# Windowed attention, first layer: score blocks of up to 256 columns two to a PSUM bank, with one exponential and one mask matmul for both

## The reference, cut to what matters

```python
# layer 0, x: (8, 512, 128)
xn = layernorm(x)
q, k, v = split(xn @ w_in.T + b_in)                 # 16 heads of 8
scores = q @ k.T / sqrt(8)                          # per head, 512 x 512
scores = where(|i - j| <= 128, scores, -1e30)
ctx  = softmax(scores) @ v
x = x + (xn + ctx @ w_out.T + b_out) + int8_matmul(xn, weight_q)
# layer 1: attention with softmax over queries, and a top-2 mixture of 8 experts
```

## Time and profile before

| | |
|---|---|
| Median of 3 runs | 592.09 us (590.72 to 592.15) |
| Span of the profiled execution | 629.5 us |
| TensorE busy in it | 526.0 us (84%) |
| VectorE busy | 442.5 us (70%) |
| ScalarE busy | 352.7 us (56%) |
| GpSimd busy | 307.6 us (49%) |
| First layer's slots, in the trace | 52 us to 353 us |

### The profile page before, as it was taken

One profiled execution on the slowest core, in us unless ns is written; L12 is line 12 of the kernel. 1 busy time (PEld: TensorE's weight loads), 2 busy tenths in 40 slices (PEclk: granted clock), 3 DMA queues, 4 the chain that ended last, 5 costly groups with the idle time before them and its releaser, 6 DMA issues. The chain is left out here.

```text
span 629.5 us, 17819 instructions
## 1 busy us (share of the span) xinstructions
PE 526.0 (84%) x5987; PEld 339.2 (54%) x5987; DVE 442.5 (70%) x1888; ACT 352.7 (56%) x995; POOL 307.6 (49%) x361
## 2 busy tenths in 40 slices
PE   5489998999999999998899898777770899999990
PEld 4124344444444444453444565555550899999890
DVE  6598898798988988887692357677564566555552
ACT  2254777777777777777477545445423145455450
POOL 6572636447465584550101054466644066666562
PEclk9555999999999999999599998778875999999997
DMA  4836073473725548174002070001111133445434
GB/s 104 178 101 135 20 175 81 119 136 87 166 74 145 112 120 163 35 174 92 18 20 59 14 290 25 31 31 34 47 35 59 47 97 89 139 137 161 117 85 124
DMA packets 51385, 61.04 MB, mean 97 GB/s; under 512 B 10001, under 2 KB 42133, under 8 KB 49696
## 3 DMA queue, kind: packets, MB, share of 16 engines
q1 hardware_dynamic: 45824, 50.26, 32.8%
q0 software_dynamic: 4320, 8.47, 4.0%
q10 hardware_dynamic: 1152, 1.18, 0.6%
HBM read 31.68 MB, written 28.39 MB: 95 GB/s over the span
## 5 line engine op out<-in xcount | busy, mean ns | idle before, releaser
L678 DVE CUSTOM_DVE_ANT_0 A<-A,band 128x320 f32<-128x320 f32 (+2 forms) x512 | 213.9, 464 | 46.6 <-PE A L855 45.7
L531 ACT ACTIVATE Pb<-SB 128x320 f32<-128x320 f32 (+2 forms) x512 | 180.5, 401 | 83.3 <-PE SB L891 78.8
L855 PE MATMUL A<-Ks,Qs 48*64 48x320 bf16 (+2 forms) x1024 | 132.7, 311 | 19.1 <-DVE mneg L678 15.9
L882 PE MATMUL SB<-Qs,Ks 50*64 50x320 bf16 (+2 forms) x1024 | 134.7, 300 | 4.7 <-ACT Pb L531 4.1
L855 PEld LDWEIGHTS A<-Ks,Qs 48*64 48x64 bf16 x1024 | 48.9, 108 | 122.3 <-DVE mneg L678 96.3
L1773 POOL DMA_INDIRECT results<-y,xt x71 | 75.9, 1069 | 60.9 <-issue 36.8
L891 PE MATMUL SB<-ends,ident 64*64 64x64 bf16 (+1 forms) x1024 | 102.0, 209 | 1.2 <-issue 1.2
L1224 POOL DMA_INDIRECT expert_rows<-pay,pos x64 | 62.1, 970 | 71.9 <-DVE pay L1407 48.6
L904 PE MATMUL PV<-Pb,Va 128*32 128x320 f32 (+2 forms) x1024 | 87.8, 416 | 0.4 <-ACT Pb L531 0.4
L1892 PE MATMUL l_S<-xT,wt 128*128 128x128 f32 x568 | 82.1, 288 | 2.3 <-ACT xT L1781 1.8
L1892 PEld LDWEIGHTS l_S<-xT,wt 128*128 128x128 f32 x568 | 68.7, 191 | 10.2 <-ACT xT L1781 2.4
(11 more groups left out here) (263 smaller groups left out, 821.6 us busy)
## 6 DMA issues: line engine op xcount, KB each, us to landing
Qs<-parts_dram SPq DMA_DIRECT2D x14, 384.0 KB, 6.0
Ks<-parts_dram SPq DMA_DIRECT2D x14, 384.0 KB, 9.6
xt<-expert_rows SPq DMA_DIRECT2D x71, 65.0 KB
yb<-results SPq DMA_DIRECT2D x7, 512.0 KB
parts_dram<-qp SPq DMA_DIRECT2D x16, 192.0 KB, 2.9
parts_dram<-kp SPq DMA_DIRECT2D x14, 192.0 KB, 2.8
xb<-in_x SPq DMA_DIRECT2D x8, 256.0 KB, 3.1
parts_dram<-qp SPq DMA_DIRECT2D x16, 128.0 KB, 2.8
```

Of the source, the lines that this page charges most:

```text
L531: act.activation(Pb[:, group % 4, c, 0:w], SB[k % NB_BANKS][:, 0:w], ACT.Exp).then_inc(act_exp, 1)
L678: nc.vector.tensor_tensor_reduce(scores_of, scores_of, band[:, skip:skip + w], -1.0, 3e38, ALU.add, ALU.min, mneg[:, step % 2, col:col + 1 ...
L855: mm = nc.tensor.matmul(A[k % NA_BANKS][out:out + HP, 0:w], Qs[b % RING][rows, a, HP * sub:HP * sub + HP], Ks[b % RING][rows, a, lo:lo + w ...
L882: nc.tensor.matmul(out[r0:r0 + HP, 0:w], Ks[b % RING][rows, a, HP * sub:HP * sub + HP], Qs[b % RING][rows, a, lo:lo + w], start=True, stop ...
```

## The change

Blocks of up to 256 columns (`sub` 0, 1, 6, 7; half of all slots) share a bank two by two: the even slot writes columns 0 to `w`, the odd one `w` to `2w`. The masks of both are added by one matmul per half of the partitions, behind the odd slot's scores, and ScalarE takes one exponential of 384 or 512 columns. A **fill** is now what a bank holds (one block or two); the semaphores `pe_B` and `act_exp` count fills, 24 in a step instead of 32.

```diff
+def paired(sub):
+    return reach(sub)[1] <= 256
+
+def fills_to(group):
+    step, sub = divmod(group, NS)
+    return STEP_FILLS * step + sum(HG // 2 if paired(i) else HG for i in range(sub))
+
+def fill_of(k):
+    group, c = divmod(k, HG)
+    return fills_to(group) + (c // 2 if paired(group % NS) else c)
...
         def exp(b, u):
...
-            act.wait_ge(pe_B, k + 1)
-            if c == 0 and group >= 4:
+            fill, w = fill_of(k), reach(group % NS)[1]
+            two = paired(group % NS)
+            if two and c % 2 == 0:
+                return
+            act.wait_ge(pe_B, fill + 1)
+            if c == int(two) and group >= 4:
                 act.wait_ge(pe_PV, group - 3)
-            w = reach(group % NS)[1]
-            act.activation(Pb[:, group % 4, c, 0:w], SB[k % NB_BANKS][:, 0:w], ACT.Exp).then_inc(act_exp, 1)
+            bank = SB[fill % NB_BANKS]
+            if two:
+                act.activation(Pb[:, group % 4, c - 1:c + 1, 0:w], bank[:, 0:2 * w].rearrange("p (n w) -> p n w", n=2),
+                               ACT.Exp).then_inc(act_exp, 1)
...
         def scores(b, u):
...
-            if k >= NB_BANKS:
-                pe.wait_ge(act_exp, k - NB_BANKS + 1)
+            if fill >= NB_BANKS and not second:
+                pe.wait_ge(act_exp, fill - NB_BANKS + 1)
...
-                nc.tensor.matmul(out[r0:r0 + HP, 0:w], Ks[b % RING][rows, a, HP * sub:HP * sub + HP],
-                                 Qs[b % RING][rows, a, lo:lo + w], start=True, stop=True)
+                nc.tensor.matmul(out[r0:r0 + HP, at:at + w], Ks[b % RING][rows, a, HP * sub:HP * sub + HP],
+                                 Qs[b % RING][rows, a, lo:lo + w], start=not second, stop=True, skip_group_check=second)
+            if two and not second:
+                return
...
+                if two:
+                    both = out[rows, 0:2 * w].rearrange("p (n w) -> p n w", n=2)
+                    end = 1 if sub < 2 else 0
+                    ends = both[:, :, w - HP:w] if sub < 2 else both[:, :, 0:HP]
+                    masks = ends16[rows, end].unsqueeze(1).to_broadcast([HP, 2, HP])
...
         def attend(step, sub):
-            pe.wait_ge(act_exp, HG * (group + 1))
+            pe.wait_ge(act_exp, fills_to(group + 1))
```

More of the change, by code:

```diff
@@ L54 @@
 NX = 6
+STEP_FILLS = 24
 def reach(s):
@@ L233, in load @@
             if g >= RING:
-                sp.wait_ge(pe_B, SLOTS * (g - RING + 1))
+                sp.wait_ge(pe_B, STEP_FILLS * STEPS * (g - RING + 1))
             for which, tile, stored in ((0, Qs, dma_pq), (1, Ks, dma_pk)):
@@ L526, in exp @@
             group, c = k // HG, k % HG
-            act.wait_ge(pe_B, k + 1)
-            if c == 0 and group >= 4:
-                act.wait_ge(pe_PV, group - 3)
-            w = reach(group % NS)[1]
-            act.activation(Pb[:, group % 4, c, 0:w], SB[k % NB_BANKS][:, 0:w], ACT.Exp).then_inc(act_exp, 1)
+            fill, w = fill_of(k), reach(group % NS)[1]
[4 more added lines that the diff above has]
+            if c == int(two) and group >= 4:
+                act.wait_ge(pe_PV, group - 3)
+            bank = SB[fill % NB_BANKS]
+            if two:
+                act.activation(Pb[:, group % 4, c - 1:c + 1, 0:w], bank[:, 0:2 * w].rearrange("p (n w) -> p n w", n=2),
+                               ACT.Exp).then_inc(act_exp, 1)
+            else:
+                act.activation(Pb[:, group % 4, c, 0:w], bank[:, 0:w], ACT.Exp).then_inc(act_exp, 1)
         def evac_pv(step):
@@ L869, in scores @@
             lo, w = reach(sub)
+            fill, two = fill_of(k), paired(sub)
+            second = two and c % 2 == 1
             if u % UNITS == 0:
                 pe.wait_ge(dma_m, 32 * (k // UNITS + 1))
-            if k >= NB_BANKS:
-                pe.wait_ge(act_exp, k - NB_BANKS + 1)
+            if fill >= NB_BANKS and not second:
+                pe.wait_ge(act_exp, fill - NB_BANKS + 1)
             if k == 0:
@@ L878, in scores @@
                 pe.wait_ge(dve_const, 10)
-            out = SB[k % NB_BANKS]
+            out = SB[fill % NB_BANKS]
+            at = w if second else 0
             for r0 in (0, HP):
                 rows = slice(r0, r0 + HROW)
-                nc.tensor.matmul(out[r0:r0 + HP, 0:w], Ks[b % RING][rows, a, HP * sub:HP * sub + HP],
-                                 Qs[b % RING][rows, a, lo:lo + w], start=True, stop=True)
+                nc.tensor.matmul(out[r0:r0 + HP, at:at + w], Ks[b % RING][rows, a, HP * sub:HP * sub + HP],
+                                 Qs[b % RING][rows, a, lo:lo + w], start=not second, stop=True, skip_group_check=second)
+            if two and not second:
+                return
             for r0 in (0, HP):
                 rows = slice(r0, r0 + HP)
-                if 1 < sub < NS - 2:
+                if two:
[3 more added lines that the diff above has]
+                    masks = ends16[rows, end].unsqueeze(1).to_broadcast([HP, 2, HP])
+                else:
                     ends = out[rows, 0:8 * HP].rearrange("p (n w) -> p n w", w=4 * HP)[:, :, 0:HP]
                     masks = ends16[rows]
-                else:
-                    ends, masks = (out[rows, w - HP:w], ends16[rows, 1]) if sub < 2 else (out[rows, 0:HP], ends16[rows, 0])
                 mm = nc.tensor.matmul(ends, ident16[rows, rows], masks, start=False, stop=True, skip_group_check=True)
@@ L1005, in _ @@
         pe.wait_ge(dma_later, LATER)
-        pe.wait_ge(act_exp, SLOTS * NB)
+        pe.wait_ge(act_exp, STEP_FILLS * NSTEP)
         tail["projections"]()
```

## The result

The changed kernel takes 586.26 us, the median of 4 runs (585.73 to 587.04), against 592.05 us (590.72 to 592.15) for the kernel before: a ratio of 0.9887 with a 95% interval of 0.9853 to 0.9921. The prediction was 586.1 us.

What follows compares the result with a forecast made beforehand. VectorE sets the pace, except where TensorE comes late with the next block. Terms of 2.1, 1.3, 1.0, 1.1 and 0.4 us sum to 5.9, rounded to 6: 592.1 becomes 586.1 us, range 582.2 to 589.8.

Steps and rivals of the forecast that it cites:

- The price of a pair: ScalarE's exponentials: a pair of 256 columns takes 599 ns, of 192 takes 493, by a line of 0.83 ns a column.
- Slots 4 to 11, 2.1 us: Batches 0 to 6: slot 11's `piece` comes 0.42 us earlier into VectorE's idle time; 2.1 us in all.
- The discount for the load: Slot 16's `Qs` and `Ks` load: in three batches only 0.15 of the 0.42 us is kept.
- The sign I gave: Slot 16: the wait of `piece` for `Ks` comes in more batches than three.
- The rival that it binds everywhere: The load at slot 16 binds in all batches, the first term is gone, 588.2 us; 12%.
- Slots 29 to 40, 1.3 and 1.0 us: Around the q and k copies: `qp` comes 0.21 us earlier (six batches), one exponential less ahead of `kp`, 0.2 (five).
- The last 48 slots, 1.1 us: Stretch without `piece`: scores no longer wait for a bank, `attend` waits for longer exponentials; 1.1 us gained (0.3 to 2.5).
- Masks, 0.4 us: Two mask matmuls fewer per pair, on the path only ahead of slots 4 and 27: 0.4 us (0 to 1.5).
- The slower rival: `attend` waits for the longer exponentials at each of 64 groups of pairs, 13.4 us lost, 599.5 us; 5%.
- The sign that I gave for being wrong: `attend` waiting for `Pb` more than before would show the prediction wrong.
- The sum: Terms 2.1 + 1.3 + 1.0 + 1.1 + 0.4 = 5.9 us, rounded to 6, giving 586.1 us.
- The clock rival: Batch 6's stretch at the lower clock goes, 582.5 us (11%), or another such stretch comes, 589.7 us (4%).

Runs made afterwards that it cites:

- The order on ScalarE alone: Kernel before, with exponentials of blocks up to 256 columns run two together at the odd slot, no shared bank: 594.10 us, ratio 1.0004.
- `e_only_4_7`: Blocks paired only at slots 4 to 7, all other slots as in the kernel before: 591.87 us, ratio 0.9998.

## Why the prediction was right, point by point

**What bounds the kernel.** VectorE sets the pace and stands only where TensorE comes late: right. Its work did not change, its stops did, by 0.82 us a batch.

**The price of a pair.** 601 and 490 ns against 599 and 493, so the line from the earlier trace rows holds to 512 columns, and the fixed part that two cost more than one is 0.19 us at 256 columns (2 x 393 - 601 ns). In the Trainium skill, "ScalarE: Activation LUTs", section "Rules for kernel authors", the fixed part is about 0.3 us, but for an ACTIVATE whose bias is a column of 128 values. The trace agrees: `qp` and `kp`, 512 columns with such a bias, take 0.69 and 0.72 us, 0.27 and 0.29 beside 512 x 0.83 ns. The exponentials have no such bias, and that price is none of theirs.

**Slots 4 to 11, 2.1 us.** 0.38 us measured in a batch (slot 11's stop), 0.39 by the kernel that pairs only there, against 0.42. The order on ScalarE alone gives it too (0.43 us left at slot 11), so here the mechanism is the one forecast. The discount for the load was mostly not needed. I kept 0.15 us in three of seven batches because the load of `Ks` was last at slot 16. It is still last there in two batches, and VectorE doesn't stop for it. (VectorE's stop of 0.80 us at slot 16 of batch 2 is behind TensorE's stop at 135.51, which ends 1.1 us after the load's last piece at 134.45.) The sign I gave, that the wait for `Ks` would come in more batches than three, was wrong. The rival that it binds everywhere is out.

**Slots 29 to 40, 1.3 and 1.0 us.** `project` of k waits 0.21 us less (0.37 to 0.16), and slot 40's stop is 0.19 shorter, against 0.21 and 0.2. The kernel that pairs only there gives 0.43 for both. The explanation was half of it, and this is the step that the prediction had wrong though its sizes fit: it put both terms down to ScalarE's shorter queue, but with the order alone slot 34's stop grows from 0.22 to 0.39 and slot 40's from 1.13 to 1.25. They need the shared bank too.

**The last 48 slots, 1.1 us.** 1.16 measured. The waits moved as forecast: those of the scores for an exponential fell from 9.1 to 4.2 us, those of `attend` rose from 1.3 to 3.6. 0.44 of the 1.16 goes when the pair is two exponentials, and the order alone gives none of it.

**Masks, 0.4 us.** A steady batch with own masks is 0.03 to 0.23 us longer in its batches and the last 48 slots 0.14 shorter. That allows 0 to 1 us in all; the median, 1.9 us above the changed kernel's, says more, with overlapping intervals. The 0.4 us is neither shown nor refuted.

**The slower rival**, `attend` waiting for the longer exponentials: `attend`'s weight loads wait 3.6 us for pairs and 3.8 for single ones in the whole kernel, 7.4 in all against 5.5 before. The sign that I gave for being wrong, that `attend` waits for `Pb` more than before, is there, but with 1.9 us and not 13.4, and 2.3 us more of such waits stand in the last 48 slots, where the forecast had counted them; a steady batch has less of them (0.4 us, 0.5 before).

**The sum.** 5.9 us was forecast and 5.8 measured, and that it is this close is partly luck. Batches 1 to 5 at 0.82, undisturbed, and the last 48 slots at 1.16 are 5.3 us. Batch 0 gave nothing, where 0.63 was forecast: beside the second profile of before, 35.37 and 35.34. There slot 11's stop did not shrink (0.54 and 0.62 us), and what slot 34's lost (0.61 to 0.40) slot 43's gained (0.36 to 0.59); why is open. In place of it came things that the sum did not hold, of both signs: the stop of 1.4 to 1.9 us in batch 1 (in the second profile with 3.4 us at half clock behind it) is no longer there, batch 6 is 1.6 to 4.1 us shorter, and stops for `l_xall` take 2.15 and 1.05 us in batches 3 and 4 and the stop at 135.51 1.2 in batch 2. In the second session the same two kernels were 8.0 us apart.

The clock rival named one of these: batch 6, the one with a stretch at the lower level, got shorter. That stretch is still there, though, and the change doesn't account for its length: 13.6 us in the first profile of before, 6.8 in its second, 6.8 in both of the changed kernel. With the statistics moved the pairs alone are worth 0.72 us in batch 6 (34.46 and 33.74). Of the 3.86 us between the first profiles the stop for `l_xall` is 1.43 (2.23 and 0.80), which leaves 1.7 for the shorter stretch; of the 1.80 between the second ones it is 0.85 (1.71 and 0.86). The window of the stretch in the changed kernel:

```profile
296.60:303.40 6.80, 6.71 (x76) 3.01 (x72) 4.67 (x26) 3.73 (x9) 2.94 (x6) 0.50 0.01 2
```

Such a stretch of 3.4 to 13.6 us begins at the end of the stop for `l_xall` or up to 4.6 us later in batch 6 of all eleven profiles whose statistics stand at slot 28, and in the three whose statistics moved batch 6 has none.

## What to carry to other kernels

Look for the stops of the engine that sets the pace, name for each the late one, and price a change only there: the batches that nothing else disturbed came out at 36.90 as forecast, while the engine that was relieved saved nearly three times what the kernel gained. A shared bank can be worth more than the saved instruction (0.53 against 0.18 us in a batch, the joint masks in the first figure); undo the two apart before crediting either. And where a difference of 1% is at stake, compare several batches of both profiles: a load with little lead, or a stop of TensorE that comes and goes, moves single batches by 1 to 3 us whatever the edit.

## What the runs showed of the hardware that was not expected

- A load of 256 KB lands in 2.5 to 3.0 us without an instruction packet of 16 KB beside it. All 18 of 84 that took longer, up to 4.9 us, had one running during the load; VectorE, ready some 2.7 us behind the issue, stood for 0.4 to 2.2 us for 14 of them.
- TensorE stops for 0.7 to 2.5 us between two instructions where the profile shows nothing that it waits for. In three of four profiles with the same list for TensorE it is the same instruction of batch 1; with 12 matmuls fewer at the start of the program the median rose by 3.6 us (596.10 beside 592.46).
- A stop of VectorE of 0.7 to 2.2 us in batch 6 was followed by 3.4 to 13.6 us at a granted clock of 0.50 in eleven of eleven profiles; of seven stops of 1.0 to 2.2 us in batches 3 and 4 one was. `e_only_4_7` is that one: 1.57 us, then 3.4 at half clock.
- One exponential of 128 x 512 in float32 takes 601 ns and two of 256 take 786, but with ScalarE not setting the pace, two instead of one cost a batch with 16 pairs only 0.18 us.
